# A windowed-attention and Fourier kernel: a new order of the stages on every engine of its software pipeline

## The chip, the cores and the metric

The kernel runs on one core of a Trainium2 chip. The metric is the device time of one execution in microseconds, where lower is better. The core has five engines that run side by side, each with its own instruction stream: TensorE (PE in the profile, with its weight loads as PEld), VectorE (DVE), ScalarE (ACT), GpSimd (POOL) and SyncE (SP, which issues the DMAs here). They meet only through semaphores. TensorE has a granted clock with two levels that show in the records, 1.2 and 2.4 GHz; a granted share of 1.0 is the upper one and 0.5 the lower one.

## What is computed

Input `x` is 8 x 256 x 256 x 64 in 32-bit floats. Layer 0 is a shifted-window attention block with 4x4 windows and 4 heads, layer 1 a moving average plus a mixing of Fourier modes along the rows. The first takes most of the time and is the part that the change touches:

```python
def layer0(x):
    qkv = windows(roll(x)) @ qkv_w.T + qkv_b
    qn = q / max(norm(q), 1e-12);  kn = k / max(norm(k), 1e-12)
    attn = softmax(qn @ kn.T * scale + bias)        # per window and head, 16 x 16
    a = (attn @ v) @ proj_w.T + proj_b
    x = x + layernorm(a) * norm1_g + norm1_b
    h = gelu(x @ fc1_w.T + fc1_b) @ fc2_w.T + fc2_b
    return x + layernorm(h) * norm2_g + norm2_b
```

(The reference also adds a mask between the regions of the shift. The shift is a multiple of the window, so every window lies inside one region, the mask is zero, and the kernel has none.)

## The kernel before

The image rows are cut into 512 groups of work (16 image rows by two strips of 32 columns). Every group goes through the same stages, and the kernel is a software pipeline written out by hand: in step k each engine works on group k for the first stages, on group k-2 for the scores, on k-4 for the projection, and so on. In the code `i0` is the group of this step and `i1` to `i7` those of one to seven steps ago. Each engine has a list of stage calls, and this list is the order of its instructions; nothing else sets it. `need` waits until a stage has been done for a group, `after` waits for the last user of a buffer. `over_groups` writes the first 16 steps out, then runs a hardware loop over the other 496 (TensorE's loop holds one step, that of ScalarE and VectorE four, GpSimd's eight) and writes out 7 closing steps.

The stages of TensorE, with the names used from here on and their lines:

- T, `turn_x`, L423: transposes the loaded group (4 matmuls of 128x128x128).
- QA and QB, `project_qkv`, L435: the two halves of the q, k, v projection, 8 records of 64x128 weights by 192 columns each. Both write the two PSUM banks `M`.
- S0 and S1, `scores`, L452: q times k for each window and head, 128 records of 32x32 weights by 16 columns for each half.
- W0 and W1, `weighted`, L474: probabilities times v, again 128 records of 32x32 by 16 for each half.
- P, `project`, L486: the output projection into bank `D1`.
- V1 and V2, `variance1` and `variance2`, L494 and L500: the variance of the two layer norms.
- F1a and F1b, `first_layer`, L510: the two halves of the MLP's first layer. Both write `M` too.
- S2a and S2b, `second_layer`, L522: the two halves of its second layer, into bank `H2`.

So `M` is written by QA, QB, F1a and F1b in turn. Between two of them it has to be read out: after QA and QB by VectorE (`qkv_out`, L774), after F1a and F1b by ScalarE (`gelu`, L663). ScalarE also swaps its function table twice a step (exponential and logarithm, L665; gelu, L674). VectorE's `normed1` and `add1` (L837, L845) make the input of the first layer. GpSimd normalises q and k, shifts and divides the probabilities. SP loads `x` for the next group as soon as T has freed the input buffer: 8 transfers of 32 KB (L318).

The order before on TensorE was S2a, T, S2b, F1a, P, S0, F1b, S1, V2, QA, V1, W0, QB, W1, and then the loop's edge.

Of the kernel before, what the change touches and what calls it, by code (L numbers as in the profile page):

```python
# [16 lines left out]
P = 128  # L17
C = 64
HEADS, HD = 4, 16
WIN = 4  # L20
# [63 lines left out]
def swin_then_fourier(nc, x, qkv_wt, qkv_b, v_b, proj_wt, proj_b, logit_scale, cpb_w1t, cpb_b1, cpb_w2t,  # L84
# [11 lines left out]
    with ExitStack() as ctx:  # L96
# [78 lines left out]
        V1, V2 = ps[:, 2, :], ps[:, 3, :]  # L175
        D1, H2, TR = ps[:, 5, :], ps[:, 6, :], ps[:, 7, :]

# [183 lines left out]
        def _(pe):  # L361
# [53 lines left out]
            def step(s, k):  # L415
                i0, i1, i2, i3, i4, i5, i6, i7, i8 = ago(s, k)

                def turn_x(g):
                    if there(g):
                        need(pe, x_in, g, 16 * 8)  # L420
                        need(pe, xT_sb, before(g))
                        for p in range(4):
                            ins = pe.transpose(TR[:, p * P:(p + 1) * P], xin[:, p, :], ident)  # L423
# [34 lines left out]
                def weighted(g, d, done):  # L458
                    if there(g):
                        if d == 0:  # L460
# [3 lines left out]
                            after(pe, (l2_sb, i6), (oT_sb, before(g)))  # L464
# [25 lines left out]
                def variance1(g):  # L490
                    if there(g):
                        need(pe, sq1_sb, g)
                        after(pe, (biased, i2), (l1_sb, before(g)))
# [31 lines left out]

                second_layer(i6, 0, fc2a_ps)
                turn_x(i0)
                second_layer(i6, 1, fc2b_ps)
                first_layer(i5, 0, fc1a_ps)
                project(i4)  # L530
                scores(i2, 0)
                first_layer(i5, 1, fc1b_ps)
                scores(i2, 1)
                variance2(i6)
                project_qkv(i0, 0, qkvA_ps)
                variance1(i4)
                weighted(i3, 0, pvA_ps)
                project_qkv(i0, 1, qkvB_ps)
                weighted(i3, 1, pvB_ps)

# [22 lines left out]
        def _(act):  # L563
# [19 lines left out]
            def step(s, k):  # L583
                i0, i1, i2, i3, i4, i5, i6, i7, i8 = ago(s, k)

                def keep_x(g):
                    if there(g):
# [4 lines left out]
                          TR.rearrange("p (n e j) -> p n j e", e=2, j=WIN), ACT.Copy).then_inc(xT_sb, 1)  # L592
# [72 lines left out]
                act.preload_act_table_set(EXP_SET)  # L665
                log2(i7)
                log_norm(i2)
                root2(i7)
                root_norm(i2)
                log1(i5)  # L670
                root1(i5)
                square(i1)
                exponent(i3)
                act.preload_act_table_set(GELU_SET)  # L674
                keep_o(i4)
                gelu(i5, 0, fc1a_ps, fc2a_ps, gelu0)
                square1(i4)
                square2(i6)
                keep_x(i0)
                gelu(i5, 1, fc1b_ps, fc2b_ps, gelu1)  # L680

# [27 lines left out]
        def _(dve):  # L709
# [56 lines left out]
            def step(s, k):  # L766
# [92 lines left out]
                bias(i2)  # L859
                turn_prob(i3)  # L860
                clamp(i1)
                maximum(i2)
                qkv_out(i0, 0, qkvA_ps, qkvA_sb)
                normed2(i6)
                qkv_out(i0, 1, qkvB_ps, qkvB_sb)
                normed1(i4)
                add1(i4)
                turn_q(i1)
                turn_k(i1)
                gain2(i6)  # L870
                sum_prob(i2)
                invert(i2)
                sum_squares(i0)
# [20 lines left out]
        def _(pool):  # L894
# [10 lines left out]
            def step(s, k):  # L905
# [74 lines left out]
                add_o2(i5)  # L980
                norm_k(i1)
                scale_norm(i1)
                shift(i2)
                norm_q(i1)
                add_o1(i0)
                expand_v(i2)
                add2(i6)
                divide(i2)
# [39 lines left out]
```

## Time and profile before

| what | us |
|---|---|
| median of 3 runs | 9567.78 |
| lowest and highest run | 9561.87, 9574.15 |
| the profiled execution, its run | 9592.97 |
| its span, first to last instruction | 9591.2 |
| TensorE busy in the span | 8979.9 |
| ScalarE, VectorE, GpSimd busy | 6253.6, 5628.4, 5156.4 |
| mean granted TensorE clock over the span | 0.945 |

The profiled execution is 25.2 us longer than the median of the timed runs. Of its span, some 7700 us are the hardware loop over the groups. A row of the chain of work says when a piece started, how long it held the chain and which line it is; "issue" in it is time in which TensorE had nothing to wait for that the profile shows.

### The profile page before, as it was taken

The numbers are of one execution on the slowest core, as the hardware profiler recorded it, in microseconds if no ns is written. First come the engines' busy times: TensorE is split into PE (matmuls) and PEld (weight loads), VectorE is DVE, ScalarE is ACT, GpSimd is POOL, SyncE is SP. The second block draws the span as 40 slices with busy tenths as digits, with TensorE's granted clock in tenths as the row PEclk, the third lists the DMA queues.
The fourth block names the chain that finished last, engine by engine and source line by source line (L and its number), as shares of the span: only waits on it lengthen the run. The fifth ranks groups of instructions, "written<-read, shape, count | busy, mean of one in ns | idle before, by whom it ended". The sixth has DMA issues, their size and how long they took to land.

```text
span 9591.2 us, 653934 instructions
## 1 busy us (share of the span) xinstructions
PE 8979.9 (94%) x291636; PEld 5472.3 (57%) x291636; DVE 5628.4 (59%) x8029; ACT 6253.6 (65%) x8530; POOL 5156.4 (54%) x5127
## 2 busy tenths in 40 slices
PE   8899999999999999999999999999999999887776
PEld 5455555555555555555555555555555555465665
DVE  1456666666666666666666666666666666422221
ACT  1467777777777777777777777777777777522221
POOL 0356666666666666666666666666666666300000
PEclk9799999999999999999999999999999999898888
DMA  3111111111111111111111111111111111299999
GB/s 101 34 30 34 35 34 31 34 35 34 34 34 34 35 30 34 35 34 34 34 35 33 31 35 34 35 34 35 34 33 32 35 34 35 78 320 329 332 318 327
DMA packets 1105191, 700.01 MB, mean 73 GB/s; under 512 B 616849, under 2 KB 1026833, under 8 KB 1100947
## 3 DMA queue, kind: packets, MB, share of 16 engines
q1 hardware_dynamic: 1100484, 564.33, 22.0%
q10 hardware_dynamic: 4608, 134.22, 3.3%
q8 instruction: 80, 1.31, 0.1%
q14 instruction: 19, 0.16, 0.0%
HBM read 412.97 MB, written 285.21 MB: 73 GB/s over the span
## 4 chain that ended last, share of the span: by engine, by line
PE 92%; DMA 3%; issue 3%; SPq 0%; DVE 0%; ACT 0%; ACTq 0%; POOL 0%; POOLq 0%; DVEq 0%
PE ps L452 14%; PE ps L522 13%; PE ps L474 13%; PE ps L510 11%; PE ps L435 9%; PE ps L550 9%; PE ps L500 6%; PE ps L494 6%; PE ps L486 5%; PE ps L423 4%; DMA out<-arena 3%; PE ps L397 1%; PE ps L388 1%; PE ps L389 1%; DMA xch<-y 0%
## 5 line engine op out<-in xcount | busy, mean ns | idle before, releaser
L663 ACT ACTIVATE arena<-ps,arena 128x1024 f32<-128x1024 f32 x1024 | 1142.0, 1115 | 1014.7 <-PE ps L510 1014.6
L935 POOL TENSOR_TENSOR arena<-arena 128x512 f32<-128x512 f32 x512 | 535.9, 1047 | 2147.8 <-ACT arena L610 2147.8
L452 PEld LDWEIGHTS ps<-arena 32*32 32x32 f32 x131072 | 1323.0, 105 | 636.7 <-issue 605.4
L474 PEld LDWEIGHTS ps<-arena 32*32 32x32 f32 x131072 | 1194.2, 103 | 545.6 <-issue 545.6
L452 PE MATMUL ps<-arena 32*32 32x16 f32 x131072 | 1455.3, 181 | 19.9 <-issue 17.4
L805 DVE TENSOR_TENSOR arena<-ps,arena 128x512 f32<-128x512 f32 x512 | 354.2, 692 | 1869.0 <-PE ps L452 1869.0
L522 PE MATMUL ps<-arena 128*64 128x512 f32 x4096 | 1283.2, 709 | 170.9 <-issue 164.4
L774 DVE TENSOR_TENSOR arena<-ps,arena 128x768 f32<-128x768 f32 x1024 | 979.1, 956 | 790.3 <-PE ps L435 790.1
L474 PE MATMUL ps<-arena 32*32 32x16 f32 x131072 | 1296.9, 186 | 36.9 <-issue 34.8
L550 PE MATMUL ps<-xch,amat 128*128 128x256 f32 x4096 | 924.8, 389 | 289.2 <-ACT arena L687 201.4
L510 PE MATMUL ps<-arena 64*128 64x512 f32 x4096 | 1162.4, 644 | 1.6 <-ACT arena L663 1.6
L921 POOL TENSOR_TENSOR arena<-arena 128x512 f32<-128x512 f32 x1024 | 1135.7, 1130 | 9.4 <-PE ps L474 9.4
L598 ACT ACTIVATE arena<-arena 128x1024 f32<-128x1024 f32 x512 | 541.2, 1057 | 878.4 <-DVE arena L774 878.4
L912 POOL TENSOR_TENSOR arena<-arena 128x512 f32<-128x512 f32 x512 | 537.8, 1050 | 979.1 <-DVE arena L845 703.3
L550 PEld LDWEIGHTS ps<-xch,amat 128*128 128x128 f32 x4096 | 787.6, 195 | 427.6 <-ACT arena L687 206.6
L435 PE MATMUL ps<-arena 64*128 64x192 f32 x8192 | 956.7, 352 | 7.0 <-DVE arena L774 3.2
L435 PEld LDWEIGHTS ps<-arena 64*128 64x128 f32 x8192 | 651.0, 188 | 412.2 <-issue 390.7
L687 ACT ACTIVATE arena<-ps 128x512 f32 x256 | 271.0, 1066 | 939.7 <-PE ps L550 611.8
L880 DVE COPY arena<-ps 128x512 f32 x256 | 267.8, 1051 | 944.6 <-PE ps L550 628.7
L976 POOL TENSOR_TENSOR ystripe<-arena 128x512 f32<-128x512 f32 x512 | 653.1, 1276 | 38.1 <-DVE arena L857 38.1
L674 ACT ACT_TABLE_LOAD x519 | 665.9, 1283 | 9.2
L665 ACT ACT_TABLE_LOAD x519 | 665.9, 1283 | 9.2
(89 smaller groups left out, 14143.7 us busy)
## 6 DMA issues: line engine op xcount, KB each, us to landing
arena<-in_x SPq DMA_DIRECT2D x4096, 32.0 KB
y<-ystripe SPq DMA_DIRECT2D x256, 512.0 KB, 5.6
amat<-mix SPq DMA_DIRECT2D x512, 256.0 KB, 3.4
xch<-y SPq DMA_DIRECT2D x512, 256.0 KB, 4.0
out<-arena ACTq DMA_DIRECT2D x32, 4096.0 KB, 27.1
mix<-amat SPq DMA_DIRECT2D x64, 256.0 KB, 2.0
wri<-in_w_real SPq DMA_DIRECT2D x64, 64.0 KB, 1.8
wri<-in_w_imag SPq DMA_DIRECT2D x64, 64.0 KB, 1.9
```

Of the source, the lines that this page charges most:

```text
L435: ins = mm(M[:, a, pl * 256:pl * 256 + 3 * C], xT[a * C:a * C + C, 2 * pp + pl, :], wqkv[a * C:a * C + C, :], start=True, stop=True, tile_ ...
L452: ins = mm(S[r, c0 + e:c0 + 32:2], qT[r, sl, q, e:64:2], kT[r, sl, q, e:32:2], start=True, stop=True, tile_position=(32 * cg, 32 * cg))
L474: ins = mm(PV[32 * h:32 * h + 32, b, c0:c0 + N], vexp[r, sl, h, :, :], pT[r, sl, h // 2, h % 2, :], start=True, stop=True, tile_position=( ...
L510: ins = mm(M[:, a, :], w1[a * C:a * C + C, kk * P:(kk + 1) * P], x1T[a * C:a * C + C, :], start=True, stop=True, tile_position=(a * C, 0))
L522: ins = mm(H2[a * C:a * C + C, :], w2[:, kk, :], hT[kk][:, a, :], start=(kk == 0), stop=(kk == 1), tile_position=(0, a * C))
L550: ins = mm(ps[:, j, k * T:(k + 1) * T], amat[j][:, r * T + k * P:r * T + (k + 1) * P], xch[j][:, r * T:(r + 1) * T], start=(r == 0), stop= ...
L663: f(hT[kk], M, ACT.Gelu, bias=b1[:, kk:kk + 1]).then_inc(done, 1)
L665: act.preload_act_table_set(EXP_SET)
L674: act.preload_act_table_set(GELU_SET)
L774: tt(qkv[ring(g, 4)][:, :, 4 * pp:4 * pp + 4, :].rearrange("p w s n -> p s w n"), M.rearrange("p a (s n) -> p (a s) n", s=2)[:, :, 0:3 * C ...
L921: tt(vexp.rearrange("p s h e d -> p (s h) e d")[:, :, e, :], qkv[ring(g, 4)][:, 2].rearrange("p s (h d) -> p (s h) d", h=HEADS), par[:, e: ...
L976: tt(ystripe[r // GPS][:, :, r % GPS, :].rearrange("p r (n j) -> p n r j", j=WIN), yg.rearrange(v, r=ROWS, j=WIN), x1o[ring(g, 4)].rearran ...
```

## The change

The change reorders the stage calls of all four compute engines, and moves a few of them to another group. On TensorE the attention product `weighted` works on `i4` and no longer on `i3`, the two halves of the second layer stand together with the projection behind them, the two halves of the scores follow each other, and the last stage of the loop is the second half of the first layer. Three PSUM banks swap owners (the transposed input now shares `D1` with the projection, the first variance gets a bank of its own, the second shares one with the attention product). The waits of `after` follow from that.

```diff
-        V1, V2 = ps[:, 2, :], ps[:, 3, :]
+        PA = ps[:, 3, :]
         D1, H2, TR = ps[:, 5, :], ps[:, 6, :], ps[:, 7, :]
+        XT, V1, V2 = D1, TR, PA
...
                 def turn_x(g):
-                        need(pe, xT_sb, before(g))
+                        after(pe, (dn1_sb, i5), (xT_sb, before(g)))
...
                 def project_qkv(g, pp, done):
                         if pp == 0:
-                            after(pe, (gelu1, i5), (qkvB_sb, before(g)))
+                            after(pe, (gelu0, i5), (gelu1, i6), (qkvB_sb, i1), (qkvA_sb, before(g)))
                         else:
-                            need(pe, qkvA_sb, g)
+                            after(pe, (qkvA_sb, i0), (gelu0, i5), (gelu1, i6), (qkvB_sb, before(g)))
...
                 def scores(g, part):
-                            after(pe, (l1_sb, i5), (biased, before(g)))
+                            need(pe, biased, before(g))
...
                 def weighted(g, d, done):
-                            after(pe, (l2_sb, i6), (oT_sb, before(g)))
+                            after(pe, (l2_sb, i7), (oT_sb, before(g)))
...
                 def project(g):
-                        need(pe, dn1_sb, before(g))
+                        after(pe, (xT_sb, i0), (dn1_sb, before(g)))
...
                 def first_layer(g, kk, done):
-                            after(pe, (qkvB_sb, i1), (gelu1, before(g)))
+                            after(pe, (gelu1, i6), (qkvB_sb, i1), (qkvA_sb, i1), (gelu0, before(g)))
                         else:
-                            need(pe, gelu0, g)
+                            after(pe, (qkvB_sb, i0), (qkvA_sb, i0), (gelu0, i5), (gelu1, before(g)))
...
-                weighted(i3, 1, pvB_ps)
+                first_layer(i5, 1, fc1b_ps)
...
-                gelu(i5, 1, fc1b_ps, fc2b_ps, gelu1)
+                gelu(i6, 1, fc1b_ps, fc2b_ps, gelu1)
```

TensorE, the end of the loop before, with the semaphores that each first instruction waits for. L494 is V1, L474 the attention product, L435 the second half of the q, k, v projection; the branch is the loop's edge:

```order
L494 MATMUL ps<-arena 128x512 [waits biased,sq1_sb]
L218 REGISTER_ALU
L474 MATMUL ps<-arena 32x16 [waits l2_sb,v1_sb,pT_sb,v0_sb]
L474 MATMUL ps<-arena 32x16 x63
L435 MATMUL ps<-arena 128x192 [waits qkvA_sb]
L435 MATMUL ps<-arena 128x192 x3
L474 MATMUL ps<-arena 32x16 [waits pvA_ps]
L474 MATMUL ps<-arena 32x16 x63
L242 REGISTER_ALU
L242 COMPARE_AND_BRANCH
```

The same place in the changed kernel, whose line numbers are one higher (L495 is V1, L436 QB, L453 the scores, L511 F1b):

```order
L495 MATMUL ps<-arena 128x512 [waits l1_sb,sq1_sb]
L436 MATMUL ps<-arena 128x192 [waits qkvA_sb]
L436 MATMUL ps<-arena 128x192 x3
L219 REGISTER_ALU
L219 REGISTER_ALU [waits kT_sb,qT_sb]
L453 MATMUL ps<-arena 32x16 [waits biased]
L453 MATMUL ps<-arena 32x16 x127
L511 MATMUL ps<-arena 128x512 [waits qkvB_sb]
L511 MATMUL ps<-arena 128x512
L243 REGISTER_ALU
L243 COMPARE_AND_BRANCH
```

The last stage ahead of the branch is two large matmuls where it was 64 small ones, and the scores are 128 matmuls in a row, behind QB.

TensorE, the top of the loop before (L522 is the second layer, L423 T, L510 F1a, L486 P):

```order
L522 MATMUL ps<-arena 64x512 [waits dn2_sb]
L522 MATMUL ps<-arena 64x512
L218 ISA
L423 MATMUL ps<-arena 128x128 [waits xT_sb,x_in]
L423 MATMUL ps<-arena 128x128 x3
L522 MATMUL ps<-arena 64x512 [waits gelu1]
L522 MATMUL ps<-arena 64x512
L218 REGISTER_ALU
L510 MATMUL ps<-arena 128x512 [waits qkvB_sb,x1_sb]
L510 MATMUL ps<-arena 128x512
```

And in the changed kernel (L424 is T, L475 the attention product, L511 F1a, L523 the second layer):

```order
L424 MATMUL ps<-arena 128x128 [waits dn1_sb]
L424 MATMUL ps<-arena 128x128 x3
L219 REGISTER_ALU
L219 REGISTER_ALU [waits v1_sb,v0_sb,pT_sb]
L475 MATMUL ps<-arena 32x16 [waits l2_sb]
L475 MATMUL ps<-arena 32x16 x63
L219 REGISTER_ALU [waits x1_sb]
L511 MATMUL ps<-arena 128x512 [waits gelu1]
L511 MATMUL ps<-arena 128x512
L475 MATMUL ps<-arena 32x16 [waits pvA_ps]
L475 MATMUL ps<-arena 32x16 x63
L523 MATMUL ps<-arena 64x512 [waits dn2_sb,gelu0]
```

The two attention products have moved from the loop's end to its top, one on each side of F1a, and the second layer stands behind them.

## Rows read from the trace of the kernel before

**Rows 1.** The page: span, and the granted clock of TensorE in 40 slices (tenths).

```profile
span 9591.2 us, 653934 instructions
...
PEclk9799999999999999999999999999999999898888
```

**Rows 2.** Chain of work over one step of the loop: start, us, what.

```profile
3003.18 1.08 PE ps L522 x4
3004.26 0.59 PE ps L423 x4
3004.85 1.01 PE ps L522 x4
3005.86 1.06 PE ps L510 x4
3006.92 1.01 PE ps L486 x8
3007.93 1.34 PE ps L452 x111
3009.27 1.06 PE ps L510 x4
3010.33 1.31 PE ps L452 x108
3011.64 1.06 PE ps L500 x2
3012.69 0.85 PE ps L435 x8
3013.55 1.06 PE ps L494 x2
3014.60 1.19 PE ps L474 x78
3015.79 0.85 PE ps L435 x8
3016.64 1.19 PE ps L474 x78
3017.83 0.36 issue
```

**Rows 3.** Waits between 500 and 8200 us: engine, line, releaser, total us, times, longest.

```profile
PE ps L522 <- issue: 163.4, 492, 0.5
```

**Rows 4.** Groups between 500 and 8200 us: busy us, mean ns, idle before.

```profile
L663 ACT ACTIVATE arena<-ps,arena 128x1024 f32<-128x1024 f32 x992 | 1106.3, 1115 | 952.7 <-PE ps L510 952.7
```

**Rows 5.** Windows: length, each engine's busy us (instructions), then granted clock, DMA share, GB/s.

```profile
500.00:8200.00 7700.00, 7522.52 (x277663) 4360.44 (x277662) 5144.83 (x7439) 5735.31 (x7934) 4991.60 (x4957) 0.97 0.15 34
...
3018.20:3033.25 15.05, 14.73 (x561) 8.65 (x561) 10.34 (x16) 11.50 (x17) 10.07 (x10) 0.99 0.08 17
3033.25:3049.77 16.52, 16.16 (x561) 9.12 (x561) 10.42 (x16) 11.67 (x17) 10.07 (x10) 0.90 0.35 79
...
3033.30:3036.70 3.40, 3.40 (x10) 1.23 (x12) 3.37 (x6) 2.96 (x4) 2.37 (x3) 0.55 0.00 0
```

**Rows 6.** Chain of work at the start of a step with a lower clock.

```profile
3033.25 1.98 PE ps L522 x4
3035.22 1.05 PE ps L423 x4
```

**Rows 7.** DMA in 40 slices between 3003.18 and 3018.20 us, tenths busy.

```profile
DMA  0000000021302130303030300000000000000000
```

**Rows 8.** Timelines of ScalarE and VectorE in the same step: start, us, instruction.

```profile
3010.38 1.11 ACT L663 ACTIVATE arena<-ps,arena 128x1024 f32<-128x1024 f32 x1 [0.64 <-PE ps L510]
3011.51 1.28 ACT L665 ACT_TABLE_LOAD   x1
...
3015.36 0.63 ACT L640 ACTIVATE arena<-arena 128x512 f32<-128x512 f32 x1
...
3013.60 0.95 DVE L774 TENSOR_TENSOR arena<-ps,arena 128x768 f32<-128x768 f32 x1
```

More of the change, by code:

```diff
@@ L492, in variance1 @@
                         need(pe, sq1_sb, g)
-                        after(pe, (biased, i2), (l1_sb, before(g)))
+                        need(pe, l1_sb, before(g))
                         mm(V1, ones, sq1, start=True, stop=True).then_inc(var1_ps, 1)
@@ L524, in second_layer @@
                         ins.then_inc(done, 1)
+                turn_x(i0)
+                weighted(i4, 0, pvA_ps)
+                first_layer(i5, 0, fc1a_ps)
+                weighted(i4, 1, pvB_ps)
                 second_layer(i6, 0, fc2a_ps)
-                turn_x(i0)
                 second_layer(i6, 1, fc2b_ps)
-                first_layer(i5, 0, fc1a_ps)
                 project(i4)
+                project_qkv(i0, 0, qkvA_ps)
+                variance2(i6)
+                variance1(i4)
+                project_qkv(i0, 1, qkvB_ps)
                 scores(i2, 0)
+                scores(i2, 1)
                 first_layer(i5, 1, fc1b_ps)
[L533 to L538, printed above, removed]
-                weighted(i3, 1, pvB_ps)
             over_groups(pe, step, 1)
@@ L591, in keep_x @@
                         f(xT.rearrange("p s (n j e) -> p (s n) j e", j=WIN, e=2),
-                          TR.rearrange("p (n e j) -> p n j e", e=2, j=WIN), ACT.Copy).then_inc(xT_sb, 1)
+                          XT.rearrange("p (n e j) -> p n j e", e=2, j=WIN), ACT.Copy).then_inc(xT_sb, 1)
                 def square(g):
@@ L665, in step @@
                 act.preload_act_table_set(EXP_SET)
+                exponent(i4)
+                log1(i5)
+                log_norm(i2)
+                root1(i5)
                 log2(i7)
-                log_norm(i2)
+                root_norm(i2)
                 root2(i7)
-                root_norm(i2)
-                log1(i5)
-                root1(i5)
+                act.preload_act_table_set(GELU_SET)
+                gelu(i6, 1, fc1b_ps, fc2b_ps, gelu1)
+                keep_x(i0)
                 square(i1)
-                exponent(i3)
-                act.preload_act_table_set(GELU_SET)
                 keep_o(i4)
                 gelu(i5, 0, fc1a_ps, fc2a_ps, gelu0)
+                square2(i6)
                 square1(i4)
-                square2(i6)
-                keep_x(i0)
-                gelu(i5, 1, fc1b_ps, fc2b_ps, gelu1)
             over_groups(act, step, 4)
@@ L857, in gain2 @@
                         ts(yg, dn2, g2, None, ALU.mult).then_inc(yg_sb, 1)
-                bias(i2)
-                turn_prob(i3)
+                turn_q(i2)
+                sum_squares(i1)
+                turn_k(i2)
                 clamp(i1)
-                maximum(i2)
                 qkv_out(i0, 0, qkvA_ps, qkvA_sb)
-                normed2(i6)
+                sum_prob(i3)
+                invert(i3)
                 qkv_out(i0, 1, qkvB_ps, qkvB_sb)
                 normed1(i4)
+                turn_prob(i3)
+                normed2(i6)
                 add1(i4)
-                turn_q(i1)
-                turn_k(i1)
+                bias(i2)
+                maximum(i2)
                 gain2(i6)
-                sum_prob(i2)
-                invert(i2)
-                sum_squares(i0)
             over_groups(dve, step, 4)
@@ L980, in step @@
                 add_o2(i5)
+                expand_v(i3)
+                divide(i3)
                 norm_k(i1)
+                add_o1(i0)
                 scale_norm(i1)
+                norm_q(i1)
+                add2(i6)
                 shift(i2)
[L984 to L988, printed above, removed]
             over_groups(pool, step, 8)
```

2 lines of the change are left out of this document (1 added, 1 removed).

## The prediction

> **What bounds the kernel now.** I read the chain of work first, because it says whether the engines wait for each other at all. Over a whole step every piece of it is TensorE, 14 stages back to back, and one piece of idle time of 0.36 us at the loop's edge [rows 2]. The step lasts 15.02 us, from 3003.18 to 3018.20. No stage waits for a semaphore. So for the loop the time is 496 steps, each the sum of TensorE's stages plus that idle time, and the other engines matter only if the new order makes TensorE wait for them.
>
> Then the clock. The page has it a little under full speed in nearly every slice [rows 1]. Between 500 and 8200 us there are 992 gelus, two a step, so 496 steps in 7700 us, or 15.52 us a step [rows 4, 5]. That is 0.50 more than the step in [rows 2]. The windows show where it goes: the step from 3018.20 took 15.05 us, the next one 16.52, with the same 561 records, at granted clocks of 0.99 and 0.90 [rows 5]. In it the clock was at its lower level for about the 3.4 us in which S2a, T and S2b ran (0.55 granted) [rows 5], and S2a took 1.98 us and T 1.05 in place of 1.08 and 0.59 [rows 2, 6]. Such a spell costs 16.52 - 15.05 = 1.47 us, so there is one in every three steps (0.50 / 1.47 = 0.34). What TensorE did just before it is the same each time: W0, QB, W1 and the idle time, that is 2.38 us of 32x32 matmuls, 0.85 of QB and 0.36 of nothing [rows 2]. The stretch S0, F1b, S1 (1.34, 1.06, 1.31) has no spell behind it.
>
> **The change, part by part.** The work is the same: the same stages for 512 groups. Four things differ.
>
> *The loop's edge.* 163.4 us of idle time over 492 steps [rows 3], 0.33 us a step or 165 us in all. Before the branch stood W1, 64 matmuls whose records start every 9 ns (1.19 us for 128), so the sequencer is busy issuing them until nearly their end and the branch is exposed. After the change it is F1b: two matmuls that take 1.06 us. The sequencer hands them over and branches while they run. I take all 165 us as gone; the bounds are 0 and 165, and the upper one is nearest since 0.36 is a third of the cover.
> The Trainium skill ("TensorE: Matmul & The Clock Gate", section "Part 1: The HAM clock gate") gives TensorE a queue of 64 instructions. By it the end of a burst would lie in the queue too, and the branch would be longer than the idle time shown. The idle time of [rows 2] behind W1 shows that such cover was not enough there; F1b's 1.06 us would still be enough.
>
> *The bursts against the loads of x.* S0 and S1 take 1.34 and 1.31 us where W0 and W1, with as many records of the same shape, take 1.19 [rows 2]. The DMA row shows when the loads of x run: slices of 0.375 us, busy from the ninth to the twenty-third, 3006.2 to 3011.8, which is over both halves of the scores and over neither half of the product [rows 2, 7]. They begin 1.35 us after T's end. In the new order T is first, so the loads run from about 1.9 to 7.5 us of the step, over part of F1a, W1 and the second layer, and the scores stand at 10.9 and later, outside. If the loads are what slows the small matmuls, the scores gain 0.15 + 0.12 = 0.27, nearly all of it taken here as 0.25, and W1 loses 0.12: 0.13 us a step, 64 us in all. The bounds are 0 (the scores are slower by themselves) and 0.27 (W1 doesn't suffer), 0 to 134 us.
>
> *The waits.* M is the buffer to watch. Gelu reads F1b out 1.16 us after its end (3010.33 to 3011.49), `qkv_out` reads QA out 1.0 us after its end [rows 8]. Cover in the new order [rows 2]: F1b to F1a has T and W0, 1.78 us; F1a to QA has W1, S2a, S2b and P, 4.2; QA to QB has V2 and V1, 2.12; QB to F1b has the scores, 2.45. ScalarE is the closest: between V1 and F1b's gelu it has its whole logarithm and exponential stretch and a table load. Before, a table load and these six instructions lasted from 3011.51 to 3015.99, 4.48 us [rows 8]; between V1's end and F1b's end TensorE has 0.85 + 2.45 + 1.06 = 4.36. Gelu may thus start 0.1 late and eats that much of the 0.6 that T and W0 leave over. I cost the waits at nothing. The step's full-speed length becomes 15.02 - 0.33 - 0.13 = 14.56 us.
>
> *The clock.* This term decides the sign. The thinnest stretch of the old order was 2.38 us of bursts, QB and 0.36 idle, 3.59 in all. It is gone: W0 and W1 now stand around F1a (1.19, 1.06, 1.19), much like S0, F1b, S1, which had no spell behind it. But the new order has QB and then both halves of the scores, 0.85 + 2.45 = 3.3 us, with no large matmul inside. The bursts alone are as long as W0, W1 and the idle time together were, and unbroken. So I expect a spell about as often as before or a little more, 0.4 a step. What follows is worse than before. The old spell fell on S2a, T, S2b and F1a, all of them large matmuls, and the clock was back after it. The new one falls on F1b, T and W0, and behind W0 come F1a and W1; F1b and T take 2.06 and 1.05 at the lower level by the ratios of [rows 6], so W0 lies inside the 3.4 us. Half-clocked TensorE with a burst in it does little, and the spell can go on over F1a and W1. I take one spell as making one more on average: 0.4 x 2 = 0.8 spells of 3.4 us a step. Half of them cost the known 1.47 us; those over W0 and W1 less, since a burst of records that start every 9 ns is bound by more than the clock, and I put them at 1.1. That is 0.8 x 1.28 = 1.03 us a step against 0.50 before, 0.53 more, or 263 us. The bounds are far apart: at the old rate and price nothing is added, and with one spell more than that in each step it is 1.5 us a step or +500.
>
> Sum: -165 - 64 + 263 = +34 us, on the median of 9568: 9602. In the profiled execution's own time that is a span of about 9625. The written-out steps at both ends do the same work and are left as they are.
>
> **Rivals.**
> 1. *The clock is not worse off* (chance 0.28). The scores are short enough without the loads that the thin stretch brings a spell no more often than before, each one ending at once. Then only the first two terms are left: 9568 - 229 = 9339, and with half of the added spells 9470. For it: the idle time itself disappears, and no burst is nearer than 0.85 us to such a gap. Against it: 2.45 us of 32x32 records in a row, twice what the old order had anywhere.
> The Trainium skill ("TensorE: Matmul & The Clock Gate", sections "Part 1: The HAM clock gate" and "Why this matters for your kernels") says that the clock falls after TensorE has been idle, and asks only that idle gaps be avoided. By it this rival would be certain. The trace speaks against the rule: the clock falls behind bursts and 0.36 us of idle time, in steps in which TensorE idles nowhere else.
> 2. *The burst is slow by itself and the clock pays for it* (chance 0.20). If the loads have no part in it, the scores stay at 2.65 and the step at full speed is 14.69; the unbroken burst is then 3.5 us with QB, and a spell a step at 1.28 makes 15.97 us, 0.45 x 496 = 223 us more: 9790. It decides from 2.6 us of burst on. For it: the scores' operands are strided in SBUF, the product's are not.
> 3. *The edge stays exposed* (chance 0.07). F1b needs VectorE's copy of QB, and if the sequencer waits there until F1b starts, little is gained. Then 165 us come back and the idle time stands right behind the scores: 9770.
> 4. *A new wait* (chance 0.05). Gelu or `add1` comes 0.2 us too late for F1a in each step: 9602 + 100 = 9700.
>
> **How the numbers follow.** The forecast, more spells that eat what the edge and the bursts give, has a chance of 0.40 and a range of its own of 9530 to 9690. A measurement of this kernel can tell 0.2% from no change, 19 us. Of the forecast's 0.40 some 0.04 lie below that band, 0.11 in it and 0.25 above. Faster: 0.28 + 0.04 = 0.32. Same: 0.11. Slower: 0.25 + 0.20 + 0.07 + 0.05 = 0.57. The range goes from the middle of rival 1 to just above rival 2, 9390 to 9810, which leaves out about one in ten at either end.
>
> **What would show it.** In the profile of the changed kernel the second layer's idle time by "issue" should be gone, and no idle time should stand at T. S0 and S1 together should last about 2.45 us and start with the DMA row empty, with W1 at 1.2 to 1.3. A step at full clock should last 14.5 to 14.6 us. The granted clock in the loop should be lower than before, with the lower level on F1b and T and going on over W0, F1a and W1. If the clock is as high as before, rival 1 holds and the forecast is wrong by its largest term; if the bursts are still slow with no DMA beside them, the second term is wrong; idle time of TensorE by a gelu or VectorE's line would be rival 4.

## The result, and the profile after

The changed kernel takes 8854.15 us (8850.95 to 8856.04, four runs) against 9566.36 for the kernel before: a ratio of 0.9254, interval 0.9238 to 0.927. It is 712 us faster. The forecast was 9602, in a range from 9390 to 9810.

The page of the changed kernel, its span and the granted clock of TensorE in 40 slices; it answers to [rows 1]:

```profile
span 8849.2 us, 652880 instructions
...
PEclk9789999999999999999999999999999999889888
```

Tenths are too coarse to show what has happened to the clock. The windows do. First the kernel before between 500 and 7000 us, then the changed one (length, busy us of PE, PEld, DVE, ACT and POOL, then granted clock, DMA share and GB/s):

```profile
500.00:7000.00 6500.00, 6348.03 (x234274) 3679.12 (x234273) 4342.66 (x6279) 4838.92 (x6693) 4213.19 (x4185) 0.97 0.15 34
```

```profile
500.00:7000.00 6500.00, 6487.51 (x258972) 4067.60 (x258960) 4901.96 (x6938) 5327.66 (x7400) 4658.45 (x4628) 1.00 0.17 37
```

The clock is now at its upper level practically all the time, and TensorE's idle time has fallen from 152 us to 12. In the same stretch the gelus went from 837 to 925, so a step takes 6500 / 462.5 = 14.05 us where it took 15.53. Over 496 steps 1.48 us are 734 us. That is more than the 712 between the medians, because the profiled execution of the kernel before is itself some 25 us longer than its median; the two profiled spans are 742 us apart.

The chain of work over one step of the changed kernel (start, us, what; L453 are the scores, L475 the product, L511 the first layer, L523 the second, L501 and L495 the variances), to be held against [rows 2]:

```profile
3001.32 2.26 PE ps L453 x215
3003.59 1.06 PE ps L511 x4
3004.64 0.59 PE ps L424 x4
3005.23 1.32 PE ps L475 x82
3006.55 1.06 PE ps L511 x4
3007.61 1.35 PE ps L475 x80
3008.96 1.87 PE ps L523 x8
3010.83 0.86 PE ps L487 x8
3011.69 0.85 PE ps L436 x8
3012.54 1.06 PE ps L501 x2
3013.60 0.86 PE ps L495 x2
3014.46 0.85 PE ps L436 x8
3015.31 2.26 PE ps L453 x214
```

The step lasts 13.99 us (3001.32 to 3015.31), and there is no idle piece in it. Beside the missing 0.36 us at the edge three stages have become shorter whose own matmuls are the same: the second layer takes 1.87 us in place of 1.08 + 1.01, P 0.86 in place of 1.01, V1 0.86 in place of 1.06. The scores take 2.26 in place of 1.34 + 1.31. Only W0 and W1 are longer, 1.32 and 1.35 in place of 1.19. So the gain has two parts. The step at full clock is 1.03 us shorter, some 510 us in all. And the low spells of the clock are gone from the loop. In the profiled execution of the kernel before they cost 0.44 us a step (15.48 us in the mean of the loop's steps against 15.04 in the steps at full clock), 219 us; in an execution of median length it is nearer 200, which is what 712 less 510 leaves.

### The profile page after: what moved, and what is told of

Same layout as the page of the kernel before. It is cut to its first block, busy times and chain, and to the rows that moved or that the text cites. A ratio compares the mean times of both kernels' runs of the same rounds, so it can differ in the third digit from the quotient of the medians.

```text
span 8849.2 us, 652880 instructions
## 1 busy us (share of the span) xinstructions
PE 8401.3 (95%) x291636; PEld 5471.0 (62%) x291636; DVE 5742.6 (65%) x8029; ACT 6230.1 (70%) x8530; POOL 5155.6 (58%) x5127
## 3 DMA queue, kind: packets, MB, share of 16 engines
q8 instruction: 80, 1.31, 0.1%
## 4 chain that ended last, share of the span: by engine, by line
PE 93%; DMA 4%; issue 1%; SPq 0%; POOL 0%; DVE 0%; ACTq 0%; ACT 0%; POOLq 0%; DVEq 0%
PE ps L475 15%; PE ps L453 13%; PE ps L511 12%; PE ps L523 11%; PE ps L436 10%; PE ps L551 10%; PE ps L501 6%; PE ps L487 5%; PE ps L495 5%; PE ps L424 3%; DMA out<-arena 3%; PE ps L398 1%; PE ps L389 1%; PE ps L390 1%; SPq L262 0%
## 5 line engine op out<-in xcount | busy, mean ns | idle before, releaser
L475 PEld LDWEIGHTS ps<-arena 32*32 32x32 f32 x131072 | 1290.9, 104 | 541.8 <-issue 508.4
L475 PE MATMUL ps<-arena 32*32 32x16 f32 x131072 | 1425.4, 186 | 17.9 <-issue 12.6
L453 PEld LDWEIGHTS ps<-arena 32*32 32x32 f32 x131072 | 1167.1, 105 | 152.6 <-issue 152.6
L453 PE MATMUL ps<-arena 32*32 32x16 f32 x131072 | 1218.9, 180 | 34.3 <-issue 34.3
L511 PE MATMUL ps<-arena 64*128 64x512 f32 x4096 | 1178.9, 652 | 8.6 <-ACT arena L664 4.5
L523 PE MATMUL ps<-arena 128*64 128x512 f32 x4096 | 1016.8, 617 | 1.8 <-DVE arena L852 1.4
L436 PEld LDWEIGHTS ps<-arena 64*128 64x128 f32 x8192 | 646.7, 187 | 596.5 <-issue 486.0
L436 PE MATMUL ps<-arena 64*128 64x192 f32 x8192 | 950.6, 351 | 9.9 <-DVE arena L775 7.2
L801 DVE STREAM_TRANSPOSE arena<-arena 128x1024 f32<-128x1024 f32 x512 | 638.2, 1246 | 487.7 <-POOL arena L945 487.7
L592 ACT ACTIVATE arena<-ps 128x512 f32<-128x512 f32 x512 | 305.9, 598 | 577.2 <-POOL arena L913 542.8
```

The lines of the kernel that those rows point to most:

```text
L436: ins = mm(M[:, a, pl * 256:pl * 256 + 3 * C], xT[a * C:a * C + C, 2 * pp + pl, :], wqkv[a * C:a * C + C, :], start=True, stop=True, tile_ ...
L453: ins = mm(S[r, c0 + e:c0 + 32:2], qT[r, sl, q, e:64:2], kT[r, sl, q, e:32:2], start=True, stop=True, tile_position=(32 * cg, 32 * cg))
L475: ins = mm(PV[32 * h:32 * h + 32, b, c0:c0 + N], vexp[r, sl, h, :, :], pT[r, sl, h // 2, h % 2, :], start=True, stop=True, tile_position=( ...
L511: ins = mm(M[:, a, :], w1[a * C:a * C + C, kk * P:(kk + 1) * P], x1T[a * C:a * C + C, :], start=True, stop=True, tile_position=(a * C, 0))
L523: ins = mm(H2[a * C:a * C + C, :], w2[:, kk, :], hT[kk][:, a, :], start=(kk == 0), stop=(kk == 1), tile_position=(0, a * C))
```

## The experiments

Each run stands beside runs of the kernel before on the same chip; these took 9574 to 9587 us, where those beside the changed kernel took 9566. So a difference of a run to the changed kernel's 8854 us is uncertain by some 10 to 20 us, while the ratios are not touched by it. Where a spell of low clock is counted, it is from the clock records of the trace, between about 560 and 7290 us, and the steps are those in the same stretch. The step at full clock is from the steps in which no spell falls. The views shown here have neither.

### The loop's edge

E1 takes the kernel before and moves nothing but the place at which the loop closes. The cyclic order of the stages is the same.

```diff
-                second_layer(i6, 0, fc2a_ps)
-                turn_x(i0)
-                second_layer(i6, 1, fc2b_ps)
-                first_layer(i5, 0, fc1a_ps)
-                project(i4)
+                project(i5)
...
-                weighted(i3, 1, pvB_ps)
+                weighted(i4, 1, pvB_ps)
+                second_layer(i6, 0, fc2a_ps)
+                turn_x(i0)
+                second_layer(i6, 1, fc2b_ps)
+                first_layer(i5, 0, fc1a_ps)
```

> The kernel before, with the same cyclic order of the stages on TensorE, but the loop's edge moved: the loop now starts with the projection and ends with F1a, so that the branch stands behind two large matmuls and W1 is followed by S2a inside the loop. Theory A (the branch is exposed behind a burst of small matmuls only, and the idle time it made was part of what brought the clock down): the 0.33 us of idle time ahead of S2a are gone, the step at full clock is 14.65 us in place of 15.03, the low spells of the clock nearly vanish (from 0.3 a step to under 0.1), and the whole is 300 to 400 us faster than before, about 9200. Theory B (the edge costs its idle time, the clock depends on the bursts alone): 165 to 190 us faster, about 9390, granted clock in the loop still 0.97. Theory C (the edge costs the same wherever it stands): no change.

It takes 9211 us, a ratio of 0.9618 (0.9598 to 0.9637), 363 us faster. From its chain of work, W1 and the second layer with no idle time between them, and then its window as above:

```profile
3012.15 1.19 PE ps L474 x78
3013.34 1.01 PE ps L522 x4
3014.35 0.59 PE ps L423 x4
```

```profile
500.00:7000.00 6500.00, 6489.12 (x246615) 3821.86 (x246619) 4569.96 (x6608) 5093.90 (x7049) 4434.27 (x4406) 0.99 0.16 36
```

Theory A holds with its size. The idle time is gone, the step at full clock is 0.40 us shorter (14.64), and the clock has 18 spells in 458 steps where it had 130 in 434. Half of what the whole change brings comes from the place of the branch alone: 0.73 us a step, 0.40 of it directly and some 0.33 through the clock. Whether the clock gained by the missing idle time itself or by the shorter step isn't separated: E7 and E11 below shorten the step to 14.75 us with the idle time in place, and they lose half of the spells too.

E2 is the reverse on the changed kernel: F1b opens the step and the branch stands behind the scores.

```diff
+                first_layer(i6, 1, fc1b_ps)
                 turn_x(i0)
...
                 scores(i2, 1)
-                first_layer(i5, 1, fc1b_ps)
```

> The changed kernel with the same cyclic order on TensorE, but the edge moved from behind F1b to behind the scores: the loop starts with F1b and ends with the second half of the scores. Theory A: 0.35 us of idle time show ahead of F1b, the step at full clock is 14.3 us in place of 13.95, and since the idle time lengthens the thin stretch of 2.26 us of scores to 2.6, low spells of the clock come back, 0.6 to 0.8 a step, for 15.2 to 15.4 us a step: about 9500, or 600 to 700 us slower than the changed kernel. Theory B (idle time alone): 175 us slower than the changed kernel, about 9030, clock at 1.00.

9001 us, 146 more than the changed kernel. The chain has its idle piece again, behind the scores:

```profile
3014.28 2.40 PE ps L453 x195
3016.68 0.21 issue
3016.89 1.13 PE ps L511 x4
```

but there is no spell at all in 471 steps. Here theory A is wrong and theory B right. 0.21 us of idle time behind a burst of scores, less than the 0.36 behind W1 before, doesn't bring the clock down. So it isn't idle time behind just any burst.

### The scores in one burst

E3 splits the scores again around F1b, with the edge left behind F1b.

```diff
+                scores(i3, 1)
                 turn_x(i0)
...
                 scores(i2, 0)
-                scores(i2, 1)
                 first_layer(i5, 1, fc1b_ps)
```

> The changed kernel with the scores' two halves on either side of F1b, as before: the loop ends with QB, S0, F1b, and S1 opens the next step. The edge stays behind F1b. Theory A (each change of the matmul's tile shape costs some 0.15 to 0.25 us, and thin stretches bring the clock down): the step at full clock is 14.1 to 14.2 us, 0.2 longer. The stretch from S0 over F1b to S1, T and W0 is now thin nearly throughout, and low spells come back, over one a step: 15.5 to 16 us a step, 9600 to 9850 in all. Theory B (the scores in one burst save only what the loads of x cost them, the clock stays): 8860 to 8950.

8994 us, 140 more than the changed kernel. At full clock the step is 14.12 us, 0.13 longer, the price of one more place at which large matmuls and small ones meet. The rest is the clock, 28 spells in 472 steps, most of them 6.8 us long. All but one of those in the loop begin on F1a, 0.07 to 0.31 us after its start, that is behind S1, T and W0. That is far from the spell in each step that A expected, and more than B allowed.

### The loads of x

E7 (the kernel before) and E8 (the changed one) leave out the loads of x in the loop.

```diff
                 for k in range(8):
-                    load_x(d * 2 + k // GPS, k % GPS, Group(d * 8, k))
...
-                        need(pe, x_in, g, 16 * 8)
+                        if isinstance(g.base, int):
+                            need(pe, x_in, g, 16 * 8)
```

> The kernel before, with the loads of x left out in the loop (only the first 16 groups are loaded; the others compute on what lies in the buffer, and TensorE doesn't wait for a load there). Theory L (the loads slow the bursts of small matmuls that run beside them): S0 and S1 last 1.20 us each in place of 1.36 and 1.34, W0 and W1 stay at 1.19, the full-clock step is 14.75. Theory R (the scores are slower by their operands): S0 and S1 stay as they are. The clock has its spells in either case, behind W0, QB, W1 and the idle time; with L about 9430, with R no change.

> The changed kernel, with the loads of x left out in the loop in the same way. Theory L: W0 and W1 last 1.19 us in place of 1.19 to 1.34 and 1.36, the scores stay at 2.26, the step is 13.7 us in place of 14.0, 110 to 150 us faster than the changed kernel: about 8725. Theory R (W1 is slower by where it stands): no change, 8855.

E7 takes 9323 us, E8 8726. Chain of work of E7, the scores with F1b between:

```profile
3012.33 1.20 PE ps L452 x113
3013.53 1.06 PE ps L510 x4
3014.59 1.20 PE ps L452 x111
```

and of E8, the product around F1a:

```profile
3004.77 1.19 PE ps L475 x79
3005.96 1.06 PE ps L511 x4
3007.02 1.19 PE ps L475 x79
```

Theory L holds in both. The loads make whichever bursts run beside them longer, by 0.29 us a step in either kernel (the step at full clock goes from 15.04 to 14.75 us in E7, from 13.99 to 13.70 in E8), so that the change gains nothing here: it frees the scores and hands the loads to W0 and W1. E7 is 107 us faster than L had it, since the spells fell to 60 in 450 steps. They still begin right behind W1, and W0, QB, W1 and the idle time last as long as before; only the step has become shorter. So the number of spells can halve with nothing changed in the work that they stand behind. I have no rule for that.

E14 uses it: in the changed kernel the loads are released by F1a's end.

```diff
-                need(sp, xT_ps, before(g))
+                if there(before(g, 6)):
+                    need(sp, fc1a_ps, before(g, 6))
+                else:
+                    need(sp, xT_ps, before(g))
```

> The changed kernel with the loads of x released by F1a's end instead of T's, so that they run beside the second layer, P, QA, V2 and V1 and beside no burst. Nothing else is changed. By the run without loads: W0 and W1 last 1.19 us each, the scores stay at 2.26, step 13.7 to 13.75, 110 to 130 us faster than the changed kernel: 8730. If the loads then land too late for the next T, or reach into the scores: 8770 to 8860.

8779 us, a ratio of 0.9169 to the kernel before (0.9153 to 0.9184), 75 us faster than the changed kernel, whose interval lies wholly above, and 49 us short of the 8730 that was expected. W0 is back at 1.19 us and W1 nearly, at 1.24 in the mean:

```profile
3004.25 1.19 PE ps L478 x79
3005.44 1.06 PE ps L514 x4
3006.50 1.19 PE ps L478 x80
```

The DMA row in 40 slices between 3002.61 and 3016.30 us, from F1b to F1b, shows a store of y at the start and the loads moved back, over the second layer, P, QA and the variances. The step is 13.81 us at full clock and not 13.70, so more than a third of the loads' price stays. W1 and the scores (2.33 us in the mean) are still lengthened in some steps; which transfer does that was not separated.

```profile
DMA  9999985000000000303021212203030300000000
```

### What a change of tile shape costs

E9 and E10 add the same spare matmul to the changed kernel, 128x128 weights by 256 columns into PSUM columns that nothing reads: in E9 between V2 and V1, which have that shape, in E10 between QB and the scores, which haven't.

```diff
                 variance2(i6)
+                mm(ps[:, 4, 256:512], ones, w1, start=True, stop=True)     (E9)
                 variance1(i4)
                 project_qkv(i0, 1, qkvB_ps)
+                mm(ps[:, 4, 256:512], ones, w1, start=True, stop=True)     (E10)
                 scores(i2, 0)
```

> The changed kernel with one spare matmul a step, 128x128 weights by 256 columns into columns of a PSUM bank that nothing reads, placed between V2 and V1, which have 128x128 weights as well. It streams 256 of the 512 columns of V1, which takes 0.86 us behind V2: 0.43 us a step. Theory A (a stage costs 0.1 to 0.25 us more where the tile shape changes ahead of it): +0.43 us a step and no more, 213 us, 9068. With a fixed cost for each further stage of 0.2 it is +0.63, 9167.

> The same spare matmul between QB (64x128 weights) and the scores (32x32), so that there is one change of tile shape more. Theory A: +0.43 and 0.2 for the change, 0.6 to 0.65 us a step, 300 to 320 us, 9165, some 100 us more than with the spare matmul between V2 and V1. If changes of shape cost nothing, both take the same. The clock stays at 1.00 in both.

9073 and 9168 us, both within 6 us of theory A. From the chains, the spare matmul in E9 (L536) and in E10 (L538):

```profile
3006.09 1.06 PE ps L501 x2
3007.15 0.43 PE ps L536 x2
3007.58 0.86 PE ps L495 x2
```

```profile
3005.30 0.85 PE ps L436 x8
3006.15 0.63 PE ps L538 x2
3006.78 2.26 PE ps L453 x216
```

The same instruction takes 0.43 us among its like and 0.63 between others: 0.20 us for the change of shape. The Trainium skill ("TensorE: Matmul & The Clock Gate", section "Part 3: Packing small matmuls — row/col tiling") says that a weight load overlaps matmuls in flight only where its row group differs. V2, the spare matmul and V1 all fill every row group, and they follow each other without the 0.20 us, so the rows don't follow from that rule alone. V2, the spare matmul and V1 also share their weights, `ones`, so here equal weights could pass for equal shape. S2a, S2b and P have different weights of one shape, and they too are shorter where they stand together (2.73 against 3.10 us for the three), so the weights needn't be equal for it.

E11 does one such pairing in the kernel before: T goes ahead of S2a, and the two halves of the second layer meet.

```diff
-                second_layer(i6, 0, fc2a_ps)
                 turn_x(i0)
+                second_layer(i6, 0, fc2a_ps)
                 second_layer(i6, 1, fc2b_ps)
```

> The kernel before with T ahead of S2a, so that the two halves of the second layer stand together; nothing else is moved. Theory A: one change of tile shape fewer, S2a and S2b last 1.77 to 1.87 us in place of 2.09, the full-clock step is 14.85, the spells of the clock stay: 70 to 120 us faster than before, about 9470. If changes of shape cost nothing: no change, or slower where T has to wait.

9318 us, a ratio of 0.973 (0.9709 to 0.9751), 258 faster and more than twice what was expected:

```profile
3020.88 0.38 issue
3021.26 0.63 PE ps L423 x4
3021.89 1.87 PE ps L522 x8
```

The pairing is there (1.87 us for both halves) and the idle time at the edge too. The step at full clock is 14.76 us, 0.28 shorter: 0.18 by the second layer and T together, and some 0.1 by S1, which with T earlier now mostly escapes the loads. Beyond that the spells went from 130 in 434 steps to 58 in 450, although W0, QB, W1 and the idle time stand as before. That was not foreseen. What follows the idle time has changed, T and not S2a, and so has the length of the step. E7 speaks for the length: it leaves T where it was, its step is as long (14.75 us), and it has as many spells (60 in 450). Two runs that agree are no proof of it.

### What brings the clock down

E5 and E6 lengthen the burst of scores by computing one or two of its eight slots twice (E15 and E16: three and four).

```diff
-                        for sl in range(part * 4, part * 4 + 4):
+                        for sl in ([0, 1][:1] if part == 0 else []) + list(range(part * 4, part * 4 + 4)):
```

> The changed kernel with one of the eight slots of the scores computed twice (16 matmuls more, 32 records, at the start of the burst), so that the burst lasts 2.53 us in place of 2.26. Theory A (the clock falls from a certain length of thin work on, between the 2.6 us that brought no spell with the edge behind the scores and the 2.9 us that did with W0 and W1 together): the clock stays at 1.00, the step is 0.27 us longer, 135 us more than the changed kernel: 8990. Theory F (the forecast: 2.45 us of scores behind QB bring 0.8 spells a step): 9250 to 9500.

> The changed kernel with two of the eight slots of the scores computed twice, a burst of 2.8 us. Theory A: low spells of the clock are back, 0.3 to 0.8 a step, granted clock in the loop 0.94 to 0.98; with 0.54 us of more work a step it takes 9250 to 9550. If the burst's length were not what matters (rival: the spells in the run with W0 and W1 together came from the T ahead of them or from the 0.14 us of idle time within them), the clock stays at 1.00 and it takes 9120.

> The changed kernel with three of the eight slots of the scores computed twice: a burst of 3.06 us, longer than the 2.92 us of W0 and W1 together that lost the clock. Theory K (any 32x32 burst over about 2.9 us brings spells): 0.3 a step or more, 9450 and up. Theory H (a burst of scores is denser work for the clock than one of the product): hardly any spells, 9185 + 135 = 9320.

> The same with four slots twice, a burst of 3.33 us. Theory K: spells in most steps, 9700 and up. Theory H: still few, 9450.

They take 9021, 9185, 9338 and 9475 us. The steps are longer by the added work, 0.27 us for each slot, and by little else: 3, 11, 17 and 14 spells in 470, 460, 451 and 443 steps. Those that begin before 640 us stand at the written-out steps; without them 0, 7, 13 and 8 are left. E6 thereby goes against theory A, which had 0.3 to 0.8 a step from 2.8 us on. The longest burst in E16's chain and its window, then the same length of window clear of the written-out steps:

```profile
3011.72 3.33 PE ps L453 x316
```

```profile
500.00:7000.00 6500.00, 6471.66 (x293118) 4224.62 (x293114) 4515.21 (x6393) 4911.74 (x6822) 4291.18 (x4263) 0.99 0.15 35
...
700.00:7200.00 6500.00, 6498.55 (x296235) 4252.36 (x296233) 4560.16 (x6457) 4957.26 (x6889) 4331.65 (x4303) 1.00 0.15 35
```

E16's step at full clock is 15.06 us, as long as that of the kernel before (15.04), and it has 8 spells where that has some 128. So whatever the length of a step does to their number, it isn't what rid the changed kernel of them.

E4 puts W0 and W1 together in the changed kernel, E17 does so with the last slot of both left out.

```diff
                 weighted(i4, 0, pvA_ps)
-                first_layer(i5, 0, fc1a_ps)
                 weighted(i4, 1, pvB_ps)
+                first_layer(i5, 0, fc1a_ps)
```

> The changed kernel with W0 and W1 next to each other and F1a behind them (T, W0, W1, F1a, S2a ...). Theory A: two changes of tile shape fewer, 0.2 to 0.35 us a step, with a burst of 2.4 to 2.5 us that begins behind T; by the scores' burst of 2.26 us, which brought no low spell, and T's large transposes ahead of it, the clock should hold: 13.75 us a step, about 100 us faster than the changed kernel, 8750. If 2.5 us of burst is already too much, low spells come back and it is slower than the changed kernel, 8900 to 9300. Theory B (changes of shape cost nothing): no change, 8855.

> The kernel with W0 and W1 together, with the last of the eight slots left out of both in the loop (an eighth of the product isn't computed), so that the burst lasts 2.55 us in place of 2.92, as long as the scores with one slot twice, which kept the clock. Theory K: no spells, the step is 13.9 us, 8790 to 8820. Theory H (the product's burst is thinner): spells stay, though fewer than the 0.35 a step of the whole one: 8900 to 9200.

E4 takes 9301 us, 447 more than the changed kernel, E17 8927. The burst in E4's chain, then its window and E17's:

```profile
3056.50 1.37 PE ps L475 x79
3057.88 0.14 issue
3058.01 1.41 PE ps L475 x75
```

```profile
500.00:7000.00 6500.00, 6372.62 (x243804) 3882.42 (x243805) 4610.00 (x6530) 4992.75 (x6970) 4378.81 (x4352) 0.96 0.16 35
```

```profile
500.00:7000.00 6500.00, 6337.84 (x242448) 3875.33 (x242446) 4860.91 (x6882) 5244.22 (x7344) 4615.90 (x4586) 0.98 0.16 37
```

E4 has 160 spells in 452 steps, E17, whose burst lasts 2.50 us, 63 in 476. The burst of scores at 2.53, 2.79, 3.06 and 3.33 us had next to none. Theory K and the forecast's F fall, and H holds as far as it says that the kind of burst matters and not its length alone: at the same length, with records of the same shape, a burst of the product brings the clock down and one of the scores hardly does.

The two bursts of that pair differ in more than their kind, though. E17's holds 224 records in its 2.50 us, E5's 288 in 2.53, and between W0 and W1 TensorE waits for W0's last result (total us, times, longest):

```profile
PE ps L475 <- PE ps L475: 142.5, 459, 0.4
```

That is 0.31 us in each step, and the scores have nothing of the kind. The wait isn't needed for a spell: in E1 W0, QB and W1 follow each other in 3.23 us with 256 records and no idle time, and 17 spells stand right behind them, while QB and the scores of E5, 3.38 us with 288 records, have none behind them after 640 us. How much of E4's and E17's many spells the wait and the fewer records account for was not tested, nor was T right ahead of them, though before the change W0, QB and W1 bring spells with no T ahead.

Two other differences between the product and the scores were tried. The expanded v has a zero in half of its places. E13 fills them in the kernel before:

```diff
-                           par[:, e:e + 1].unsqueeze(2).to_broadcast([P, 32, HD]), ALU.mult).then_inc(done, 1)
+                           par[:, e:e + 1].unsqueeze(2).to_broadcast([P, 32, HD]), ALU.add).then_inc(done, 1)
```

> The kernel before, with the expanded v filled everywhere: its two copies are masked by adding the 0 or 1 of the mask in place of multiplying by it, so that no half of the weights of W0 and W1 is zero (the output is another). Theory G: the values don't matter, the spells stay at 0.3 a step, 9570. Theory Z (the zeros in the weights are what made TensorE look idle in W0 and W1): the spells go, step 15.03, 9340.

9570 us, a ratio of 0.9994 (0.9984 to 1.0005), 119 spells in 436 steps. The zeros have no part in it that shows.

The other difference is which 32-row strips of the array are in use. A half of the product uses strips 0 and 2 or 1 and 3, each with four column strips; the scores go round all four. E12 gives a long burst of scores the product's order over the rows:

```diff
-                                    for cg in range(4):
+                        for pair in ((0, 2), (1, 3)):
...
+                                        for cg in pair:
```

> The changed kernel with the longer burst of scores (two of eight slots computed twice, 2.8 us), in which the same matmuls stand in another order: within each half first all those on row strips 0 and 2 of the array, then all on 1 and 3, as the product's halves have them, in place of going round all four strips. Theory G (a burst on two of the four strips counts as thin work for the clock, one on all four doesn't): low spells come back, 0.2 to 0.8 a step where the same burst over four strips had 11 spells in 460 steps; 9250 to 9600 in all. Theory Z (the product's bursts bring the spells for another reason): the clock stays, and if the rate of the records stays too it takes 9185.

12186 us, a clock of 0.75 in the loop:

```profile
3008.63 6.35 PE ps L454 x313
```

(This one runs partly at the lower level.) The run doesn't decide the question. The burst takes 5.05 us at full clock where it took 2.79, since with two tiles in turn the records come at 15.8 ns and no longer at 8.7, so it changes length and rate along with the strips. That such a burst brings spells in every step agrees with theory G, and with thin work of any kind. Whether the row strips in use are what the clock goes by stays open.

## Why the prediction was wrong, point by point

**What bounds the kernel** was read rightly: TensorE back to back, and the time is 496 steps of it. So was the size of the loss by the clock, 0.50 us a step where the loop's steps show 0.44, and where its spells fall.

**The loop's edge** was right: 165 us forecast and 0.33 to 0.40 us a step found in E1. With the clock, moving the edge was worth 363 us by E1. The forecast had that gain in its clock term, where the thinnest stretch "is gone" and the old 0.50 us a step are taken off, but put 1.03 us of new spells in its place.

**The bursts against the loads** was right as a mechanism and wrong by its sum. The scores gained 0.29 us (E7) and W0 and W1 together lost 0.29 (E8), not 0.12. I had only W1 beside the loads; W0 is hit as well in many steps. The forecast's 64 us are about zero, the lower end of its bounds. (The working also has the scores at 2.45 us where 2.65 less 0.25 is 2.40, which changes nothing.)

**A term was missing.** The step at full clock was to be 14.56 us and is 13.99. The forecast took the stages' times from [rows 2] as if they were the stages' own. In fact each time at which the tile shape changes from one stage to the next contains some 0.2 us for that change (E9 against E10: 0.43 and 0.63 us). The new order has fewer changes: S2a, S2b and P follow each other with one shape, V2 and V1 with another, and the scores are entered once. That is 1.08 + 1.01 + 1.01 - 1.87 - 0.86 = 0.37, 1.06 - 0.86 = 0.20 and 0.13 (E3), 0.7 us a step by these pieces, or nearly 350 us. With the loads at zero and the edge's 0.33 to 0.40 they make the 1.03 us. The text's first sentence on the change, that the work is the same and four things differ, is the step that failed. [Rows 2] could have shown it: F1a has one matmul of 512 columns on each half of the rows and takes 1.06 us, QA has two of 192 on each half and takes 0.85. That is 0.21 us for 128 columns, 1.64 ns each, so 512 columns are worth 0.84 us, and 0.2 us of each stage belong to no column.

**The clock** was the largest term and had the wrong sign: +263 us forecast, some -200 found. The step that failed is "the bursts alone are as long as W0, W1 and the idle time together were, and unbroken. So I expect a spell about as often". It takes a burst of scores and one of the product to be alike for the clock, since their rows look alike. The forecast's 0.4 new spells a step were none in the changed kernel's loop. E5, E6, E15 and E16 show that the scores' burst brings hardly any spells even at 3.33 us; E4 and E17 show that the product's, with its wait inside, does at 2.5. The hint was in [rows 2] and was read too weakly: S0, F1b, S1 (3.71 us with 2.65 of burst) never had a spell behind it, and W0, QB, W1 and 0.36 us (3.59 with 2.38 of burst) had one in every third step. It was put down to the idle time and to F1b, not to the kind of burst. What in the kind of burst does it stays open. The second half of the argument, that a spell would go on over W0 and W1, was never put to the test in the changed kernel, which has no spells in its loop; E3's begin on F1a ahead of W1 and are mostly of 6.8 us, and so at least agree with it. Its upper bound doesn't come out of its own terms: one spell a step more than the old 0.34, at 1.28 us each, is 1.7 us a step, some +600 us and not +500.

**The rivals.** Rival 1 was on the right side with a clock that isn't worse off, though not for its reason, a burst that is short enough: E16 keeps the clock with 3.33 us. Its 9339 still lacked the changes of shape and the spells that vanish. Rival 2's premise is refuted by E7: the scores aren't slow by themselves. Rival 3 is refuted by the missing idle piece. Rival 4: VectorE and ScalarE never hold TensorE up in the changed kernel's step; the costing of the waits at nothing was right. The rule of the Trainium skill ("TensorE: Matmul & The Clock Gate", sections "Part 1: The HAM clock gate" and "Why this matters for your kernels") that idle gaps are what to avoid would have made rival 1 certain. Its side was right, but idle time doesn't sort these runs: E2 has 0.21 us of it in each step and no spell, E4 has some 0.25 and 160 spells, and E1 has none at the edge and 18.

## What to carry to other kernels

Where TensorE bounds a loop of many small stages, try an order in which stages with the same tile shape stand together and the loop's branch comes behind a few long matmuls, and don't read a stage's time in the chain as its own: it holds the change from the stage ahead of it. In this kernel the low spells of the clock belonged to one kind of thin work and not to another of the same length, so test which one before pricing a new order by the length of its bursts. Put transfers beside large matmuls rather than beside bursts of small ones where you can (75 us in E14).

## What the runs showed of the hardware that was not expected

- A change of tile shape between neighbouring matmuls costs 0.20 us (0.43 against 0.63 us for the same instruction), at full clock and with its inputs long ready.
- Moving the branch from behind a burst of small matmuls to behind two large ones shortened the step by 0.40 us directly and by some 0.33 through fewer low spells (E1).
- The number of low spells can halve with the work ahead of them unchanged: 130 in 434 steps of 15.04 us, 60 and 58 in 450 steps of 14.75 us (E7, E11).
- 32x32 matmuls on four diagonal tiles in turn come every 8.7 ns per record, on two tiles in turn every 15.8 ns (E12).
- Loads of 32 KB that have nothing to do with the running matmuls lengthen the bursts beside them by 0.29 us a step (E7, E8), while the large matmuls beside them keep their 1.06 us.
- Bursts of the same record shape differ for the clock: 3.33 us of scores (384 records) brought 14 spells in 443 steps, 2.50 us of the product (224 records with 0.31 us of waiting among them) 63 in 476. The zeros in the weights are not the cause (E13); the cause is open.
